# Attention over a latent context, one core: where VectorE takes the reciprocal of the row sums in its queue

## The reference

```
q_hk   = (hidden_q @ Wq.T).reshape(b, s, H, K)              # H = 16 heads
q_big  = einsum('bshk,hkq->bshq', q_hk, w_kc_q)
kv_rope = kv_c * cos + rotate_half(kv_c) * sin              # context: 512 keys of 64 values
q_r    = einsum('bshq,hqr->bhsr', q_big, W_qr)
k_r    = einsum('bld,hdr->bhlr', kv_rope, W_kr)
scores = einsum('bhsr,bhlr->bhsl', q_r, k_r)
attn   = softmax(scores, axis=-1)
ctx_c  = einsum('bhsl,bld->bhsd', attn, kv_rope)
out    = einsum('bhsd,hkd->bshk', ctx_c, w_kc_kv).reshape(b, s, H * K) @ Wo.T
x      = x + out
```

## Time and profile before

| | |
|---|---|
| median of 3 runs | 2960.64 us (2959.87 to 2961.27) |
| time of the profiled execution | 2961.07 us, its span 2959.2 us |
| granted TensorE clock, mean over the span | 0.869 |
| busy: PE, DVE, ACT, POOL | 2425.8 (82%), 1737.1 (59%), 1008.2 (34%), 769.9 us (26%) |
| the three latent loops, start of the first scores to the last sum into x | 897.67 to 1139.45, 1999.64 to 2241.49, 2517.66 to 2759.81 us |

### The profile page before, as it was taken

One profiled execution on the slowest core, in us unless ns is written; L12 is line 12 of the kernel. 1 busy time (PEld: TensorE's weight loads), 2 busy tenths in 40 slices (PEclk: granted clock), 3 DMA queues, 4 the chain that ended last, 5 costly groups with the idle time before them and its releaser, 6 DMA issues. The chain is left out here.

```text
span 2959.2 us, 37118 instructions
## 1 busy us (share of the span) xinstructions
PE 2425.8 (82%) x14074; PEld 1610.9 (54%) x14074; DVE 1737.1 (59%) x3519; ACT 1008.2 (34%) x2293; POOL 769.9 (26%) x573
## 2 busy tenths in 40 slices
PE   7797343486999997977979797889998887999899
PEld 4555222123434555665858586755557765555555
DVE  5435678696435664278696969525665763565311
ACT  3032001362105552124545453415552131555210
POOL 1120001000007883300000000008881000888322
PEclk8788555697999998987888989789999969999999
DMA  1000000003000001041010101030001004000311
GB/s 35 19 21 22 0 0 14 0 0 107 1 0 1 1 1 58 1 147 27 30 29 30 29 30 29 2 100 1 1 1 43 21 1 100 1 1 1 118 36 39
DMA packets 98937, 81.29 MB, mean 27 GB/s; under 512 B 51504, under 2 KB 90272, under 8 KB 98185
## 3 DMA queue, kind: packets, MB, share of 16 engines
q1 hardware_dynamic: 97737, 77.47, 9.2%
q0 software_dynamic: 1024, 1.45, 0.2%
HBM read 73.56 MB, written 5.35 MB: 27 GB/s over the span
## 5 line engine op out<-in xcount | busy, mean ns | idle before, releaser
L2017 POOL TENSOR_SCALAR work<-work,small 128x512 f32<-128x512 f32 x384 | 594.3, 1566 | 706.6 <-DVE small L1952 705.3
L1995 ACT ACTIVATE work<-psum,small 128x512 f32<-128x512 f32 x384 | 260.6, 683 | 254.6 <-DVE small L1947 254.6
L1947 DVE TENSOR_REDUCE small<-psum 128x2 f32<-128x1024 f32 x192 | 234.7, 1224 | 176.0 <-PE psum L1897 176.0
L1907 PEld LDWEIGHTS psum<-consts,work 128*128 128x128 f32 x1536 | 165.4, 141 | 113.8 <-issue 102.1
L1897 PE MATMUL psum<-keysT,arena_a 64*128 64x512 f32 x768 | 219.2, 650 | 8.9 <-ACT work L1995 6.0
L1919 PE MATMUL psum<-work,keys 128*64 128x256 f32 x1536 | 187.0, 384 | 36.9 <-issue 34.3
L1907 PE MATMUL psum<-consts,work 128*128 128x128 f32 x1536 | 211.3, 281 | 3.5 <-DVE work L1958 2.6
L1919 PEld LDWEIGHTS psum<-work,keys 128*64 128x64 f32 x1536 | 120.0, 136 | 136.7 <-issue 110.8
L2849 PE MATMUL psum<-xnT,arena_a 128*128 128x256 f32 x512 | 138.2, 425 | 24.7 <-DVE arena_b L3269 23.8
L1958 DVE COPY work<-psum 128x512 f32<-128x512 f32 x192 | 130.9, 682 | 19.7 <-PE psum L1907 19.7
L2002 ACT ACTIVATE work<-psum 128x512 f32<-128x512 f32 x192 | 114.4, 596 | 71.8 <-PE psum L1907 71.8
(11 more groups left out here) (589 smaller groups left out, 4992.5 us busy)
## 6 DMA issues: line engine op xcount, KB each, us to landing
arena_b<-alpha_rows SPq DMA_DIRECT2D x16, 512.0 KB, 5.7
arena_a<-in_L_xattn_Wo SPq DMA_DIRECT2D x3, 2048.0 KB, 14.6
arena_a<-in_L_xattn_Wq SPq DMA_DIRECT2D x3, 2048.0 KB, 12.7
arena_a<-in_L_xattn_w_kc_q SPq DMA_DIRECT2D x3, 1536.0 KB, 12.2
arena_a<-in_L_attn_w_qkv SPq DMA_DIRECT2D x1, 4096.0 KB
arena_a<-in_L_xattn_W_qr SPq DMA_DIRECT2D x3, 768.0 KB
arena_b<-in_L_ffn_w_fc SPq DMA_DIRECT2D x1, 2048.0 KB
arena_b<-in_L_ffn_w_proj SPq DMA_DIRECT2D x1, 2048.0 KB
```

Source lines behind the costliest of these rows:

```text
L1907: mm = nc.tensor.transpose(ps[:, 4 + j, c * P:(c + 1) * P], probs[u % NPB][:, j, c * P:(c + 1) * P], k.c["ident"])
L1947: nc.vector.tensor_reduce(top[:, 2 * u:2 * u + 2], ps[:, u % 2 * 2:u % 2 * 2 + 2, :], AX.X, ALU.max, negate=True).then_inc(*maxed.up())
L1995: nc.scalar.activation(probs[u % NPB][:, j, :], ps[:, u % 2 * 2 + j, :], ACT.Exp, bias=top[:, i:i + 1], accum_out=total[:, i:i + 1]).then_ ...
L2017: nc.gpsimd.tensor_scalar(probs[u % NPB][:, j, :], probs[u % NPB][:, j, :], total[:, i:i + 1], None, ALU.mult).then_inc(*scaled.up())
```

## The change

In the DVE's list of the latent loop, the two first entries of a step change places: in step s it takes the reciprocals of unit s-1 before the row maxima of unit s, where it took them after. Nothing else is different: the same instructions, buffers, semaphores and counts, on every engine. The wait of `invert(s - 1)` for the exponentials of unit s-1 now stands ahead of `row_max(s)`. In step 0 there is no reciprocal and in steps 64 to 71 no maximum, so 63 steps of each loop differ.

```diff
             for s in range(U + LAG + 5):
+                if 0 <= s - 1 < U:
+                    invert(s - 1)
                 if s < U:
                     row_max(s)
-                if 0 <= s - 1 < U:
-                    invert(s - 1)
                 q = (s - LAG - 2) // 2
                 if s % 2 == 1 and 0 <= q < U // 2:
                     keep_sums(q)
```

## The result

The changed kernel takes 2971.64 us (median of 6 runs, 2969.15 to 2979.14), the kernel before 2960.26 us beside it (6 runs, 2958.35 to 2965.09): ratio 1.0042, 95% interval 1.0029 to 1.0054, 11 us slower. The forecast was 2968.1 us with a range of 2964.5 to 2974.0. The profiled execution was the longest of the six, 2979.14 us with a span of 2977.3 us, so its span must not be compared with that of before; its loops can. All executions of all kernels here count as fast but one, of 5547.01 us, of the kernel with the new order from step 6 on; it is left out of that kernel's ratio.

The account below looks back on a forecast made before the run. The bound was a 7.37 us steady chain through PE, VectorE and ACT, without reciprocals or GpSimd. Start delays of 2.63, 2.56 and 2.26 us sum to 7.45; 2960.64 + 7.45 = 2968.1 us, range 2964.5 to 2974.0.

Parts of the forecast that it names:

- first five units: Start of each loop: units 0 to 4 run one by one, first over_keys late by 2.63, 2.56 and 2.26 us.
- steady steps: Even and odd steps after the start: the new order costs 0 and a pair stays at 7.37 us.
- Links of 2.81 us: Loop start: maxima, exponentials, reciprocal and next maxima follow in series, 1.26 + 1.48 + 0.07 = 2.81 us.
- 0.14 us to spare: Odd steady steps: maxima could start at 1020.89 us behind the reciprocal, while PE lets them start at 1021.03.
- a slip of 0.79 us: Odd steady steps: ACT's 0.65 us of idleness also covers late maxima; only a slip beyond 0.79 us reaches the path.
- second slow stretch: Loop start, around over_keys: PE's low clock again, up to 1.75 us a loop, 5.3 in all; 0 in the sum.
- the start costs more, by the clock: Rival at the loop starts: PE's clock makes the start cost more, 2970 to 2974 us; 13 in 100.
- stages outside the loops: Everything outside the three latent loops: nothing is edited there, so no cost was counted.
- made-good delay: Rival in the steady pairs: PE's 0.39 us idle per pair swallows the delay, 2960.6 to at most 2964 us; 17 in 100.
- gain from early reciprocals: Rival in the steady pairs: GpSimd's 1.18 us wait per pair goes, saving 96 us, 2865 us; 4 in 100.
- reciprocal held up by GpSimd: Rival in every step: reciprocal waits for a GpSimd tile, up to 0.8 us a pair, 70 us, 3030 us; 6 in 100.
- the old chain: Steady pair: scores, maxima, exponentials, ACT's copy, over_keys, transposition and next scores close in 7.37 us without slack.

Follow-up runs that it names:

- four copies: Changed kernel plus four 128 x 2 constant copies on VectorE between reciprocal and maxima of every step; ratio 1.0045 to the kernel before.
- sixteen copies: Changed kernel plus sixteen 128 x 2 constant copies on VectorE between reciprocal and maxima of every step; 3136.72 us, ratio 1.0574 to the kernel before.
- start-only kernel: Kernel before, with the new order only in steps 0 to 5 of each loop; 2974.04 us, ratio 1.0040.
- delay-only kernel: Kernel before, order unchanged, with two further maxima into unused columns ahead of each loop's first maxima; ratio 1.0030 (third loop alone 1.0007, first alone 1.0005).
- second measurement: The changed kernel run and profiled once more without any edit; ratio 1.0038 to the kernel before.
- faster kernel: Kernel before, with ACT's copy keep(s-3) put ahead of the exponentials in even steps; 2923.72 us, ratio 0.9859; with the changed order too, 0.9911.

## Why the prediction was right

**The place of the cost.** In the loops it was forecast in the first five units of each, with nothing in the steady steps and at the end. Shown by the two halves of the change: the start alone has the changed kernel's loops and ratio, the rest alone those of before.

**Its size in the loops.** Links of 2.81 us were forecast and 2.80 to 2.82 measured; from first maxima to over_keys 14.59 and 14.53. The first over_keys was forecast late by 2.63, 2.56 and 2.26; it was late by 2.57, 2.51 and 2.20, and the loops lasted 2.53, 2.44 and 2.16 longer. Sum 7.45 forecast, 7.13 in the first profile and 7.4 in the second.

**Steady steps.** 0.14 us to spare in odd steps was forecast, 0.13 seen, and that a slip of 0.14 us beyond it is free was shown with four copies. I had put the limit at a slip of 0.79 us and tested nothing close to it. The sixteen copies showed another limit, the ring of two links, that the prediction did not name. A label in the prediction is wrong and changes no number: the unit whose tiles GpSimd ends near 1022.57 and PE transposes at 1025.34 is e-3, since `turn` runs three steps behind, and not e-1.

**TensorE's clock.** I kept up to 1.75 us a loop for a second slow stretch. It did come: in the changed kernel's first loop the low clock lasts some 6.9 us, about twice the time of the earlier trace rows,

```profile
904.30:907.10 2.80, 1.33 (x4) 0.30 (x4) 1.29 (x2) 1.45 (x4) 2.52 (x2) 0.65 0.00 0
907.10:909.20 2.10, 2.07 (x5) 0.57 (x6) 1.28 (x2) 0.78 (x3) 2.10 (x2) 0.50 0.00 0
909.20:912.60 3.40, 3.40 (x14) 2.08 (x14) 1.88 (x3) 2.05 (x8) 3.40 (x4) 0.59 0.00 0
```

and ends before over_keys at 916.10. It cost nothing that can be seen in this loop: the start took 14.53 us, and the links of VectorE and ACT that set its pace are as long as forecast. At most 0.4 us a loop was seen in any start with the new order and no other edit (14.90 in the first loop of the start-only kernel, where the low stretch began about 1 us later).

**The number itself was in part luck.** The time rose by 11.4 us where 7.45 were forecast, and 2971.64 us lies in the 2970 to 2974 of the rival "the start costs more, by the clock". That rival's mechanism did not add to the starts: they took 14.53 us and not up to 16.3. The range held the result because it was wide for another reason. The term that failed is the stages outside the loops, which the prediction put at 0 since nothing is edited there. It is taken up under "What stays open".

**The rivals.** The made-good delay fell with the delay-only kernel. The gain from early reciprocals fell with both kernels that have the new order from step 6 on. A reciprocal held up by GpSimd fell too: over the changed kernel's span it takes 147 to 167 ns, with GpSimd at work beside it. In that the trace again does not bear out, for the reciprocal, the exclusive lock of which the Trainium skill tells (SBUF — State Buffer, "Who interferes with whom"). The copies that I added are of a kind that it names, and they were held: with sixteen of them the step lost 0.42 us (1.58 for 1.16) where GpSimd's tile ran beside them. Not all were held to the tile's end; the one of 0.60 us ends near 1021.6, the tile at 1022.47.

**What stays open.** The ratio says 11 to 12 us (0.42%, and 0.38% in the second measurement), the loops 7.1 to 7.4. The interval of one ratio is 3.7 us either way, so one such difference is little. But all three measurements with the new order at the start and no other edit lie above their loops, by 5.3, 3.9 and 4.4 us. The kernel with four copies lies 2.7 above its loops, and on the faster kernel, with ACT's copy first, the new order costs 15.1 us for 6.5 in the loops. The six kernels without the new order at the start, delayed or not, lie between 0.8 below and 0.9 above theirs. Chance is a poor explanation of that.

The mean granted clock of the executions points at where it is. In the first group it is 0.8687 for the kernel before, 0.8658 and 0.8649 for the changed and the start-only kernel, but 0.8689 with the delay alone. From it follows an estimate of the time at the low level, 2 x (1 - clock) x span: 20 and 26 us more than before for those two, 27 for the new order on the faster kernel, 11 with four copies, and between 6 less and 2 more for the six without it. The longer low stretches in the three starts are 10 us of that. But for the kernel with four copies, some 10 to 17 us of low clock are left for the stages outside the loops, where they cost 5 to 8 us if TensorE sets the pace throughout. That is the size of what is missing. The two profiles of the changed kernel fit: outside the loops they differ by 13 us at mean clocks of 0.864 and 0.870.

So the missing 4 to 5 us go with a lower clock outside the loops. Why the new order at the start brings it and a delay of the same length does not, no run shows. No stage can be named either: the part behind the third loop was longer in the profiles of the changed and the start-only kernel (201.5, 204.2, 203.8 us for 200.1), but also in two of the delay-only ones (204.1 and 202.6), whose times are not above their loops.

## What to carry to other kernels

An order that costs nothing in the steady state can still cost at the loop's start, where the engines are not yet spread over several units: work out the first few steps by themselves, since a delay there stays nearly whole when the steady chain has no slack. Before asking what an edit of a waiting engine is worth, close the chain of one period row by row; here it left out the reciprocals and GpSimd, and it named a copy whose move is worth 42 us. A moved wait also closes new rings: with sixteen copies the pair was two links of such a ring, 8.76 us, and not the old chain with its slips added, 8.3. And an edit can cost time where nothing was edited, here some 4 us, so compare the mean clocks of the executions as well as the edited loops.

## What I had not expected of the hardware

Small copies between SBUF tiles on VectorE follow each other at 0.07 us, and 128 x 2 is enough for them to be held up by GpSimd: sixteen took 1.16 us without its tile beside them and 1.58 with it, and its tile took 1.64 us instead of 1.56. Reciprocals of the same size were not held (147 to 167 ns). And one program's stages outside the loops differed by 13 us (2233.5 and 2246.5) between two profiles, at mean clocks of 0.870 and 0.864, where each loop repeated within 0.3 us.
